# High one-hots and low rows made three steps before their read instead of two, in a ring of eight buffers instead of six

## The chip, the core and the metric

The kernel runs on one core of a Trainium2 chip. A core has five engines that run their own instruction streams and meet only at semaphores: TensorE (PE in the rows; PEld is its loading of weights), VectorE (DVE), ScalarE (ACT), GpSimd (POOL) and SyncE (SP), which here issues most transfers. The metric is the device time of one execution, in microseconds (us).

## The reference

A recommendation model scores 2048 users. Each has 200 history positions with three item ids (below 1000) and one target item.

```python
ub = jnp.concatenate([table_i1[rec_his[:, :, 0]], table_i2[rec_his[:, :, 1]], table_i3[rec_his[:, :, 2]]], axis=2)
mask = rec_his[:, :, 0] == 0
q = jnp.broadcast_to(item_emb[:, None, :], ub.shape)
att_in = jnp.concatenate([q, ub, q - ub, q * ub], axis=-1)
h = att_in @ w_att1.T + b_att1
score = (h @ w_att2.T + b_att2)[..., 0]
score = jnp.where(mask, 0.0, score)
browse = jnp.einsum('bl,ble->be', score, ub)
feat = jnp.concatenate([item_emb, browse, user_emb], axis=-1)
x = _dice(feat @ w1.T + b1, a1, g1, be1)
x = _dice(x @ w2.T + b2, a2, g2, be2)
x = jax.nn.sigmoid(x @ w3.T + b3)
```

The tables have rows of 32 numbers. `_dice` normalises over the whole batch and gates the result.

## The kernel before

**The idea.** No history row is gathered. For a user the score is linear in the looked-up rows, so a table of scores per id is made by matmuls and looked up. An id is split into a high digit (0 to 39) and a low digit (0 to 24). A one-hot matrix of the high digits, multiplied on TensorE with the user's score table, picks 25 candidates per feature; a maximum picks the low digit.

**Tiles, steps, slots.** The batch is cut into 16 tiles of 128 users. A tile is 16 steps of 8 users (16 half-histories of 100 positions), a step is two slots. All loops are over tiles; tile 0 and the last one are written out, VectorE and GpSimd loop over the tiles between, ScalarE and SyncE over pairs of them, TensorE is written out in full. The order on each engine is fixed by hand, and every step n of a tile goes like this:

1. VectorE makes `onehot_hi` (`onehot_high`, L1015: the digits compared with 1 to 40), ScalarE writes eight further columns of the same buffer (`lo_rows`, L902). Both do it for step n + AHEAD while they work on step n; AHEAD is 2.
2. SyncE waits for both, and for a free buffer of `hiT`, and issues a transposing transfer `hiT<-onehot_hi` (`turn_hi`, L336). `hiT` is a ring of four, one per step.
3. TensorE in slot s reads: 24 matmuls `sel<-scoretab,hiT` (`read_scores`, L548). It waits for `hiT`, for the chunk of `scoretab`, and for VectorE and ScalarE to have finished with slot s - 2.
4. VectorE takes maxima (`pick`, L1029), ScalarE makes the low one-hot (`onehot_low`, L883).
5. GpSimd cuts the score into three bf16 parts (`split`, L441 to L457), VectorE multiplies them with the low one-hot (`scale`, L1041).
6. TensorE five slots (LAG) after the read adds up: 24 matmuls `wsum_ps<-scaled_lo,onehot_hi` (`add_scores`, L565). They read the same `onehot_hi` buffer once more, so it comes free only then. ScalarE copies the sums out (L773).

VectorE's order in a step n is pick(2n), one-hot for n + AHEAD, pick(2n + 1), scale(n - 1). In slot s TensorE reads, does one piece of other work if there is one (transposes for the next tile, the first layer, a part of the browse sum, L661), adds for slot s - 5, and then does one piece of the next tile's score tables (L577, L584), for which it waits on ScalarE's copies (L780). Those pieces lie in slots 2 to 10 and 16 to 27.

**The ring before.** `onehot_hi` has six buffers. Steps 0 to 14 use five of them in turn, step 15 has the sixth. Whoever writes a buffer waits until the adds of its last user are done (`wsum_full`, L900 and L1013): at step n this is the add of slot 2n - 5, which TensorE does right after the read of slot 2n.

**SyncE's queue.** Beside the transposes it issues, every two steps, three transfers that place a chunk of the next score table (`place_scores`, L352). The first chunk of tile t + 1 is issued at step 14 of tile t, ahead of the transpose of (t + 1, 0). Every wait of SyncE holds up all that is behind it. In the last tile, at step 11, it issues one load of 1.4 MB (L379).

**Start and end.** VectorE clears `onehot_hi`'s rim (L1098) before it makes `mapq` (L1107), which TensorE needs for the first query; from that hang the first score tables (21 groups of matmuls with a ScalarE copy each, L584, L577 and L780), their placing, and the first read. After the last tile come the statistics and the two layers over the whole batch.

Of the kernel before, what the change touches and what calls it, by code (L numbers as in the profile page):

```python
# [17 lines left out]
def build(nc, r_user, r_item, r_his, table_user, table_i1, table_i2, table_i3, w_att1, b_att1,  # L18
# [22 lines left out]
    STEPS = 16  # L41
    SLOTS = 32
    PER = 16
    RING = 6
    CHUNK = 16
    CHUNKS = TILE // CHUNK
    HELD = 4
# [5 lines left out]
    with ExitStack() as ctx:  # L53
# [15 lines left out]
        weightsum = sb("weightsum", [128, 4, LO, TILE // 4])  # L69
        onehot_hi = sb("onehot_hi", [POSP, RING, PER, HJ], BF16)  # L70
        onehot_lo = sb("onehot_lo", [POS, 2, PER, U], BF16)
# [120 lines left out]
        wsum_full = sem("wsum_full")  # L192
# [24 lines left out]

        def ring_slot(n):

            return n % 5 if n < STEPS - 1 else RING - 1  # L220

        def sums_before(k, n):

            return 2 * k - (8 if 5 <= n < STEPS - 1 else 10 if n < 5 else 2 * STEPS - 2)

        def ring_used(k, n):

            return not isinstance(k, int) or sums_before(k, n) > 0

        prologue = (["attw"] + [("tableT", i) for i in range(7)] + [("digit", 1, 0), ("digit", 0, 0), "item", "query",
                                                                    "w1T", "w1uT", "w2T"])
# [44 lines left out]
                split_at[len(split_at) + (2 if r < 3 else 7)] = (r, piece)  # L278
        SPLIT_DONE = 3 * NR
        LAG = 5  # L280
        AHEAD = 2
        N_SMALL = 2 * NF + 1 + 3 + 8
        EARLY = 3
        assert TILES % 2 == 0
# [6 lines left out]
        def _(sp):  # L291
# [69 lines left out]
            def tile(t, odd, last=False):  # L361
                for n in range(STEPS):
                    if n >= 14 and not last:
                        place_scores(t + 1, n - 14, 1 - odd)
                    if n + AHEAD < STEPS:
                        turn_hi(t, n + AHEAD)
                    elif not last:
                        turn_hi(t + 1, n + AHEAD - STEPS)
                    if n % 2 == 0 and n // 2 + 2 < CHUNKS:
# [373 lines left out]
        def _(act):  # L743
# [143 lines left out]
            def lo_rows(t, n):  # L887

                k = t * STEPS + n
                hb, g0 = n // 8, (n % 8) * PER  # L890
                if n in (0, 8):

                    if isinstance(t, int) and t == 0 and n == 0:
                        act.wait_ge(task_copied, DIGITS0)
                    elif n == 0:
                        act.wait_ge(task_copied, tasks_start(t))
                    else:
                        act.wait_ge(task_copied, task_before(t, 3) + 1)

                if ring_used(k, n):  # L900
                    act.wait_ge(wsum_full, sums_before(k, n))
                act.activation(onehot_hi[0:POS, ring_slot(n), :, 1:1 + 2 * NF],  # L902
                               low_rows[:, hb, g0:g0 + PER, :, :].rearrange("p g j i -> p g (j i)"), ACT.Copy
                               ).then_inc(lo_rows_ready, 1)
# [98 lines left out]
        def _(dve):  # L1003
            def onehot_high(t, n):

                k = t * STEPS + n
                hb, g0 = n // 8, (n % 8) * PER
                if n == 0:
                    dve.wait_ge(task_copied, DIGITS0 - 1 if isinstance(t, int) and t == 0 else tasks_start(t) - 1)
                elif n == 8:  # L1010
                    dve.wait_ge(task_copied, task_before(t, 2) + 1)

                if ring_used(k, n):  # L1013
                    dve.wait_ge(wsum_full, sums_before(k, n))
                dve.tensor_tensor(onehot_hi[0:POS, ring_slot(n), :, HB:].rearrange("p g (j v d) -> p g j v d", j=NF, d=2),  # L1015
                                  digits[:, hb, g0:g0 + PER, :, :].unsqueeze(3)
                                  .to_broadcast([POS, PER, NF, HI // 2, 2]),
                                  iota_hi[:, :].rearrange("p (v d) -> p v d", d=2).unsqueeze(1).unsqueeze(1)
                                  .to_broadcast([POS, PER, NF, HI // 2, 2]),
                                  ALU.is_equal).then_inc(hi_ready, 1)  # L1020
# [194 lines left out]
```

## Time and profile before

| | |
|---|---|
| time, median of 3 runs | 1570.45 us (1567.71 to 1574.2) |
| the profiled execution: time / span | 1565.89 us / 1564.1 us |
| TensorE matmul busy | 1303.5 us, 83% |
| VectorE busy | 1227.8 us, 78% |
| ScalarE busy | 1043.1 us, 67% |
| GpSimd busy | 1006.5 us, 64% |
| TensorE's clock, granted share | 0.941 |
| transfer queue of SyncE (q1) | 162.61 MB, 52.9% of the 16 DMA engines' span |

The profile shows one execution. In its list of groups a row says which line of the kernel, which engine and operation, output and inputs with their shapes, how often, the time busy and the mean of one, and then how long the engine had been idle just before and who released it. The reads begin at 47.2 us and the last one starts at about 1502 us, so 512 slots take 1455 us. An engine's idle time costs something only where it cannot be made up later; with four engines each between 64 and 83% busy, this has to be read place by place.

### The profile page before, as it was taken

Reading aid. Unit: us, or ns where it says so; the run is one execution under the profiler, and the core shown is the slowest. Engines: PE = TensorE matmul, PEld = TensorE weight load, DVE = VectorE, ACT = ScalarE, POOL = GpSimd, SP = SyncE. Lnnn points to the kernel's source line nnn. Section 1 sums busy time; section 2 is a strip of 40 time slices with the busy share of each in tenths; the row PEclk is TensorE's granted clock in tenths of the full one; section 3 lists DMA queues with packets and bytes.
Section 4 is the critical chain, followed back from the end, with each engine's and each line's share of the span. In section 5 each row is a group of like instructions: output and inputs, shape, how many; then the busy total and the mean of one; then the engine's idle time right before and its main releaser. Section 6 shows DMA issues by size and latency. Waiting matters only on the chain.

```text
span 1564.1 us, 67116 instructions
## 1 busy us (share of the span) xinstructions
PE 1303.5 (83%) x27007; PEld 1205.9 (77%) x27007; DVE 1227.8 (78%) x1143; ACT 1043.1 (67%) x2017; POOL 1006.5 (64%) x1671
## 2 busy tenths in 40 slices
PE   5688979879798887989788897989889798988864
PEld 4577868778797876878788787878878797877861
DVE  6588868777878887887877887787788878889845
ACT  6676667766667775676767666676766767775427
POOL 3577657665767766676765766777576666767630
PEclk8899989989999999999989999999999999999976
DMA  3476666566556667666765666667666566766730
GB/s 54 104 143 131 127 117 131 124 131 135 120 127 145 127 131 125 134 135 113 137 137 128 146 127 123 126 147 126 131 144 130 130 125 141 128 129 155 142 69 1
DMA packets 517516, 194.46 MB, mean 124 GB/s; under 512 B 485445, under 2 KB 493237, under 8 KB 517245
## 3 DMA queue, kind: packets, MB, share of 16 engines
q1 hardware_dynamic: 499654, 162.61, 52.9%
q10 hardware_dynamic: 15448, 26.51, 6.8%
q8 instruction: 216, 3.54, 1.0%
q0 software_dynamic: 2144, 1.36, 0.7%
q14 instruction: 54, 0.44, 0.1%
HBM read 8.45 MB, written 1.44 MB: 6 GB/s over the span
## 4 chain that ended last, share of the span: by engine, by line
POOL 47%; issue 27%; PE 10%; ACT 5%; DVE 4%; DMA 3%; POOLq 2%; ACTq 1%; SPq 0%; DVEq 0%
POOL score L443 17%; POOL score L448 8%; POOL score_r L452 7%; POOL parts L456 4%; PE sel L548 3%; POOL parts L453 3%; POOL parts L449 3%; POOL item_rows L421 3%; PE wsum_ps L565 2%; DMA hiT<-onehot_hi 2%; POOL user_rows L429 2%; ACT scores_b L780 2%; PE misc L661 2%; DVE scaled_lo L1041 1%; DVE score_j L1029 1%
## 5 line engine op out<-in xcount | busy, mean ns | idle before, releaser
L883 ACT ACTIVATE onehot_lo<-sel,one 100x600 bf16<-100x600 f32 x512 | 389.0, 760 | 427.7 <-DVE score_j L1029 417.7
L443 POOL TENSOR_TENSOR score<-score_j 100x16 f32<-100x16 f32 x256 | 363.2, 1419 | 396.0 <-DVE score_j L1029 394.0
L548 PE MATMUL sel<-scoretab,hiT 128*128 128x75 bf16 x12288 | 543.6, 203 | 78.5 <-DMA hiT<-onehot_hi 65.6
L548 PEld LDWEIGHTS sel<-scoretab,hiT 128*128 128x128 bf16 x12288 | 509.8, 101 | 123.4 <-DMA hiT<-onehot_hi 70.7
L1029 DVE TENSOR_REDUCE score_j<-sel 100x24 f32<-100x600 f32 x512 | 398.0, 777 | 220.3 <-PE sel L548 217.4
L1041 DVE TENSOR_TENSOR scaled_lo<-onehot_lo,parts 100x3648 bf16<-100x3648 bf16 x256 | 526.3, 2056 | 15.1 <-POOL parts L456 10.4
L565 PE MATMUL wsum_ps<-scaled_lo,onehot_hi 100*128 100x75 bf16 x12288 | 528.3, 201 | 8.6 <-issue 4.4
L565 PEld LDWEIGHTS wsum_ps<-scaled_lo,onehot_hi 100*128 100x128 bf16 x12288 | 488.2, 100 | 15.4 <-issue 5.6
L1015 DVE TENSOR_TENSOR onehot_hi<-digits,iota_hi 100x1920 bf16<-100x1920 bf16 x256 | 297.8, 1164 | 59.1 <-PE wsum_ps L565 56.1
L780 ACT ACTIVATE scores_b<-acc 128x512 bf16<-128x512 f32 (+1 forms) x318 | 255.4, 803 | 35.3 <-issue 18.2
L773 ACT ACTIVATE wsum_ring<-wsum_ps 128x300 f32<-128x300 f32 x512 | 219.9, 430 | 17.1 <-PE wsum_ps L565 16.5
L448 POOL TENSOR_TENSOR score<-score,score_j 100x16 f32<-100x16 f32 x256 | 160.9, 628 | 22.4 <-POOL score L443 0.5
L577 PE MATMUL acc<-scores_b,minus_identb 128*128 128x512 bf16 (+1 forms) x212 | 101.1, 477 | 80.8 <-ACT scores_b L780 80.5
L452 POOL TENSOR_TENSOR score_r<-score,parts 100x16 f32<-100x16 f32 x256 | 145.0, 566 | 20.0
L584 PE MATMUL acc<-queryT,tableT 97*128 97x128 f32 x758 | 117.8, 299 | 40.8 <-ACT scores_b L780 40.8
L584 PEld LDWEIGHTS acc<-queryT,tableT 97*128 97x128 f32 x758 | 99.2, 203 | 45.9 <-ACT scores_b L780 45.8
L456 POOL TENSOR_TENSOR parts<-score_r,parts 100x32 bf16<-100x32 f32 x256 | 107.0, 418 | 20.1
L661 PE MATMUL misc<-weightsum,table_blk 128*96 128x128 f32 x800 | 112.9, 284 | 4.6 <-DMA weightsum<-wsum_ring 4.6
L661 PEld LDWEIGHTS misc<-weightsum,table_blk 128*96 128x96 f32 x800 | 93.3, 167 | 4.8 <-issue 4.8
L577 PEld LDWEIGHTS acc<-scores_b,minus_identb 128*128 128x128 bf16 x212 | 20.6, 97 | 92.6 <-ACT scores_b L780 91.2
L421 POOL DMA_INDIRECT item_rows<-in_L_rec_table_i_dram,ids_now x51 | 70.5, 1383 | 22.2 <-POOL ids_now L415 13.1
L902 ACT ACTIVATE onehot_hi<-low_rows 100x96 bf16<-100x96 bf16 x256 | 74.0, 290 | 0.0
(173 smaller groups left out, 760.6 us busy)
## 6 DMA issues: line engine op xcount, KB each, us to landing
scoretab<-scores_b SPq DMA_DIRECT2D x384, 93.8 KB
weightsum<-wsum_ring ACTq DMA_DIRECT2D x128, 125.0 KB
weightsum<-wsum_ring ACTq DMA_DIRECT2D x64, 150.0 KB
raw<-in_r_rec_his_dram SPq DMA_DIRECT2D x32, 150.0 KB
hiT<-onehot_hi SPq DMA_TRANSPOSE x256, 4.0
x_rows<-x_tile SPq DMA_DIRECT2D x14, 100.0 KB
scores_b<-x_rows SPq DMA_DIRECT2D x1, 1400.0 KB
item_rows<-in_L_rec_table_i_dram,ids_now POOLq DMA_INDIRECT x51
```

What stands on the lines that cost most here:

```text
L443: pool.tensor_tensor(score_2[:, :], score_j[:, p2, :, 0], score_j[:, p2, :, 1], ALU.add).then_inc(parts_step, 1)
L448: pool.tensor_tensor(score[:, :], score_2[:, :], third, ALU.add)
L452: pool.tensor_tensor(score_r[:, :], score[:, :], parts[:, p2, :, 0, 0], ALU.subtract)
L548: mm = pe.matmul(sel[:, 2 * (s % 2) + q, (c % 4) * W:(c % 4 + 1) * W] .rearrange("p (j v) -> p j v", j=NF), hiT[0:HJ, s // 2 % 4, g * POSP ...
L565: mm = pe.matmul(wsum_ps[:, s % 2, b * W:(b + 1) * W].rearrange("p (j v) -> p j v", j=NF), hi_columns(ring_slot(n), g), scaled_lo[:, n % 2 ...
L661: mm = pe.matmul(misc[0:E, 0:TILE].rearrange("p (w b) -> p w b", w=4), table_blk[:, lo, :, :].rearrange("p j e -> p (j e)"), weightsum[0:H ...
L773: act.activation(wsum_ring[:, (s // 8) % 2, :, 4 * (s % 8):4 * (s % 8) + 4], wsum_ps[:, s % 2, 0:4 * W].rearrange("p (b u) -> p u b", b=4) ...
L780: act.activation(scores_b[:, odd, :, stage, slice(*ROUNDS[r])], split_bank(first, r), ACT.Copy).then_inc(split_copied, 1)
L883: act.activation(onehot_lo[:, n % 2, g0:g0 + 8, 0:W].rearrange("p (q c) u -> p q c u", q=2), sel[0:POS, 2 * (s % 2):2 * (s % 2) + 2, 0:4 * ...
L1015: dve.tensor_tensor(onehot_hi[0:POS, ring_slot(n), :, HB:].rearrange("p g (j v d) -> p g j v d", j=NF, d=2), digits[:, hb, g0:g0 + PER, :, ...
L1029: dve.tensor_reduce(score_j[:, n % 2, g0:g0 + 8, :].rearrange("p (q c) j -> p q (c j)", q=2), sel[0:POS, 2 * (s % 2):2 * (s % 2) + 2, 0:4 ...
L1041: ins = dve.tensor_tensor(scaled_lo[:, n % 2, :, :, :].rearrange("p q i (u d) -> p (q i) u d", d=2), onehot_lo[:, n % 2, :, :].unsqueeze(2 ...
```

## The change

The constant AHEAD goes from 2 to 3 and RING from 6 to 8. The ring becomes regular (`n % 8`), and the wait for a free buffer becomes the adds of eight steps back. AHEAD stands in five loops or positions: VectorE's order (L1059 to L1064 and L1120), ScalarE's (L921, L952), SyncE's (L365, L382). Each engine's kinds of instructions stay in the same places; what changes is for which step a one-hot, its low rows and its transpose are. Before tile 0 there are three of each instead of two, and at the end of the last tile three steps without them instead of two. The transposes' own wait for a free `hiT` buffer (L335) is the read of the step before the current one instead of the one before that.

```diff
-    RING = 6
+    RING = 8
...
         def ring_slot(n):
 
-            return n % 5 if n < STEPS - 1 else RING - 1
-
-        def sums_before(k, n):
-
-            return 2 * k - (8 if 5 <= n < STEPS - 1 else 10 if n < 5 else 2 * STEPS - 2)
-
-        def ring_used(k, n):
-
-            return not isinstance(k, int) or sums_before(k, n) > 0
-
-
+            return n % RING
+
+        def ring_used(k):
+
+            return not isinstance(k, int) or k >= RING
...
-        AHEAD = 2
+        AHEAD = 3
...
-                if ring_used(k, n):
-                    act.wait_ge(wsum_full, sums_before(k, n))
+                if ring_used(k):
+                    act.wait_ge(wsum_full, 2 * (k - RING) + 2)
...
-                if ring_used(k, n):
-                    dve.wait_ge(wsum_full, sums_before(k, n))
+                if ring_used(k):
+                    dve.wait_ge(wsum_full, 2 * (k - RING) + 2)
```

VectorE before tile 0, in the kernel before: the clearing of the ring's rim, the first one-hots, the first pick (`score_j<-sel`).

```order
L1098 MEMSET onehot_hi 16x6144
L1099 MEMSET hiT 128x4x8
L1100 MEMSET onehot_lo 100x32
L1103 MEMSET onehot_hi 100x96
L1104 MEMSET onehot_hi 100x96
L1107 TENSOR_SCALAR mapq<-identf,vcol 96x96
L1110 MEMSET scoretab 128x3600 x2
L1116 COPY scoretab<-far 8x16x25 x12
L1015 TENSOR_TENSOR onehot_hi<-digits,iota_hi 100x16x120 x2
L1055 SCALAR_TENSOR_TENSOR digits_b<-raw,digit_hi 128x300
L1029 TENSOR_REDUCE score_j<-sel 100x24
```

The same place in the changed kernel, whose lines stand six lower:

```order
L1092 MEMSET onehot_hi 16x8192
L1093 MEMSET hiT 128x4x8
L1094 MEMSET onehot_lo 100x32
L1097 MEMSET onehot_hi 100x128
L1098 MEMSET onehot_hi 100x128
L1101 TENSOR_SCALAR mapq<-identf,vcol 96x96
L1104 MEMSET scoretab 128x3600 x2
L1110 COPY scoretab<-far 8x16x25 x12
L1009 TENSOR_TENSOR onehot_hi<-digits,iota_hi 100x16x120 x3
L1049 SCALAR_TENSOR_TENSOR digits_b<-raw,digit_hi 128x300
L1023 TENSOR_REDUCE score_j<-sel 100x24
```

The memset grows from 6144 to 8192 elements a partition, ahead of `mapq`, and a third one-hot is made before the first pick.

SyncE from its last load before tile 0 on, in the kernel before: transposes, and the placing of score tables.

```order
L327 DMA raw<-in_r_rec_his_dram 128x300
L336 DMA_TRANSPOSE hiT<-onehot_hi 128x16x112 x2
L352 DMA scoretab<-scores_b 40x1200 x6
L336 DMA_TRANSPOSE hiT<-onehot_hi 128x16x112
L352 DMA scoretab<-scores_b 40x1200 x3
```

And in the changed kernel:

```order
L321 DMA raw<-in_r_rec_his_dram 128x300
L330 DMA_TRANSPOSE hiT<-onehot_hi 128x16x112 x3
L346 DMA scoretab<-scores_b 40x1200 x6
L330 DMA_TRANSPOSE hiT<-onehot_hi 128x16x112
L346 DMA scoretab<-scores_b 40x1200 x3
```

From here on the pattern of the two queues is the same, but each transpose stands for one step later. So where a tile ends, the transpose between the first and second chunk of the next tile's scores is that of its step 1, no longer that of its step 0.

SyncE at the end of the last tile, in the kernel before; `scores_b<-x_rows` is the load of 1.4 MB.

```order
L352 DMA scoretab<-scores_b 40x1200 x3
L336 DMA_TRANSPOSE hiT<-onehot_hi 128x16x112
L379 DMA scores_b<-x_rows 100x2x1792
L336 DMA_TRANSPOSE hiT<-onehot_hi 128x16x112 x2
L392 DMA out_dram<-table_blk 1x2048
```

And in the changed kernel:

```order
L346 DMA scoretab<-scores_b 40x1200 x3
L330 DMA_TRANSPOSE hiT<-onehot_hi 128x16x112
L373 DMA scores_b<-x_rows 100x2x1792
L330 DMA_TRANSPOSE hiT<-onehot_hi 128x16x112
L386 DMA out_dram<-table_blk 1x2048
```

One transpose instead of two stands behind the load.

## Rows read from the trace of the kernel before

**Rows 1.** The page's groups: the one-hots on VectorE.

```profile
L1015 DVE TENSOR_TENSOR onehot_hi<-digits,iota_hi 100x1920 bf16<-100x1920 bf16 x256 | 297.8, 1164 | 59.1 <-PE wsum_ps L565 56.1
```

**Rows 2.** Waits, whole span: us in total, times, longest us.

```profile
DVE score_j L1029 <- PE sel L548: 217.4, 170, 13.9
PE sel L548 <- DMA hiT<-onehot_hi: 65.6, 26, 7.4
...
DVE onehot_hi L1015 <- PE wsum_ps L565: 56.1, 64, 1.8
...
DVE scaled_lo L1041 <- POOL parts L456: 10.4, 23, 1.8
```

**Rows 3.** Timeline where tile 2 begins: start us, us, instruction, [idle before <-releaser].

```profile
217.62 1.74 SPq L336 DMA_TRANSPOSE hiT<-onehot_hi  x1
...
218.68 1.01 PE L548 MATMUL sel<-scoretab,hiT 128*128 128x75 bf16 x24
...
220.37 0.76 ACT L883 ACTIVATE onehot_lo<-sel,one 100x600 bf16<-100x600 f32 x1 [1.52 <-DVE score_j L1029]
...
222.20 2.10 DVE L1041 TENSOR_TENSOR scaled_lo<-onehot_lo,parts 100x3648 bf16<-100x3648 bf16 x1
...
227.77 1.70 PE L548 MATMUL sel<-scoretab,hiT 128*128 128x75 bf16 x24 [7.07 <-DMA hiT<-onehot_hi]
...
229.51 0.78 DVE L1029 TENSOR_REDUCE score_j<-sel 100x24 f32<-100x600 f32 x1 [5.21 <-PE sel L548]
```

**Rows 4.** Timeline where tile 7 begins.

```profile
687.08 0.76 ACT L883 ACTIVATE onehot_lo<-sel,one 100x600 bf16<-100x600 f32 x1 [1.52 <-DVE score_j L1029]
...
689.48 1.61 PE L548 MATMUL sel<-scoretab,hiT 128*128 128x75 bf16 x24 [2.07 <-DMA hiT<-onehot_hi]
...
694.72 0.46 PE L655 MATMUL misc<-item_now,mapq 97*97 97x128 f32 x2 [0.88 <-ACT item_now L827]
```

**Rows 5.** Timeline of VectorE: first pick of tiles 1, 3, 6, 8, 10, 11, 12, 15.

```profile
133.14 0.78 DVE L1029 TENSOR_REDUCE score_j<-sel 100x24 f32<-100x600 f32 x1 [1.15 <-PE sel L548]
...
323.54 0.78 DVE L1029 TENSOR_REDUCE score_j<-sel 100x24 f32<-100x600 f32 x1 [3.73 <-PE sel L548]
...
602.08 0.78 DVE L1029 TENSOR_REDUCE score_j<-sel 100x24 f32<-100x600 f32 x1 [5.76 <-PE sel L548]
...
785.24 0.78 DVE L1029 TENSOR_REDUCE score_j<-sel 100x24 f32<-100x600 f32 x1 [1.88 <-PE sel L548]
...
967.92 0.78 DVE L1029 TENSOR_REDUCE score_j<-sel 100x24 f32<-100x600 f32 x1 [3.12 <-PE sel L548]
...
1057.02 0.78 DVE L1029 TENSOR_REDUCE score_j<-sel 100x24 f32<-100x600 f32 x1 [0.26 <-PE sel L548]
...
1149.20 0.78 DVE L1029 TENSOR_REDUCE score_j<-sel 100x24 f32<-100x600 f32 x1 [0.95 <-PE sel L548]
...
1419.34 0.78 DVE L1029 TENSOR_REDUCE score_j<-sel 100x24 f32<-100x600 f32 x1 [0.82 <-PE sel L548]
```

**Rows 6.** Timeline of the last tile's steps 12 to 14.

```profile
1479.85 1.70 PE L548 MATMUL sel<-scoretab,hiT 128*128 128x75 bf16 x24 [3.46 <-DMA hiT<-onehot_hi]
1480.19 0.86 SPq L379 DMA_DIRECT2D scores_b<-x_rows  x1
...
1481.59 0.78 DVE L1029 TENSOR_REDUCE score_j<-sel 100x24 f32<-100x600 f32 x1 [2.11 <-PE sel L548]
...
1493.29 0.43 PE L565 MATMUL wsum_ps<-scaled_lo,onehot_hi 100*128 100x75 bf16 x4 [4.44 <-issue]
...
1496.28 0.78 DVE L1029 TENSOR_REDUCE score_j<-sel 100x24 f32<-100x600 f32 x1 [4.39 <-PE sel L548]
```

**Rows 7.** The chain that ended last, first 62 us: start us, us, what.

```profile
16.23 5.19 DVE onehot_hi L1098
```

**Rows 8.** The tile hiT over the whole span: time from issue to landing.

```profile
DMA to landing us min/median/max: 3.5/4.0/8.2
```

**Rows 9.** The tile score_r on GpSimd: duration ns min/median/max, first and last start.

```profile
L452 POOL TENSOR_TENSOR score_r<-score,parts x256: 223/226/1219, 52.4 to 1505.8; 100x16 f32<-100x16 f32 x128
```

## The prediction

> **What bounds the kernel now.** I read the waits of the whole span first. TensorE waits 65.6 us in 26 pieces for the transposed one-hots, up to 7.4 us at a time; VectorE waits 56.1 us in 64 pieces, at most 1.8 us each, for TensorE's adds before it may write a one-hot buffer; and VectorE waits 217.4 us for TensorE's reads [rows 2]. The change goes at the first two: the transpose gets a step more of time, and the bigger ring ends the wait for adds (at step n it now asks for slot 2n - 9, long done, where it asked for slot 2n - 5, which TensorE is just doing). The question is which part of them the end of the kernel sees.
>
> Then I read the timeline where a tile begins. In the last steps of a tile TensorE has nothing but reads and adds, and VectorE is the slower of the two. Where tile 2 begins, ScalarE's low one-hot for the last but one slot ends at 220.37 + 0.76 = 221.13; that is what the first read would wait for if nothing else held it. VectorE's last product before it ends at 222.20 + 2.10 = 224.30. But the read starts at 227.77, after 7.07 us of idle time on TensorE, because the transpose issued at 217.62 has only now landed, and VectorE's next pick starts at 229.51, after 5.21 us of idling [rows 3]. So of TensorE's 7.07 us the pipeline pays 5.21: VectorE had work to do for the rest. Where tile 7 begins, the same wait is 2.07 us, and the read could have started at 687.08 + 0.76 = 687.84 instead of 689.48 [rows 4]; there VectorE goes on without a gap that the timeline prints. So a start of a tile costs what VectorE idles before its first pick, not what TensorE idles.
>
> **The change part by part.**
>
> *Tile starts.* The idle times before the first pick are 1.15, 3.73, 5.76, 1.88, 3.12, 0.26, 0.95 and 0.82 at eight starts [rows 5] and 5.21 at tile 2 [rows 3]: 22.9 us. The 0.26 is the largest of the seven small ones; the six others are at most that, 1.1 us by my adding of their rows, so 24.0 us over 15 starts. With the transpose issued a step earlier (VectorE needs 4.77 us of work for a step: two picks of 0.78 [rows 5], a one-hot of 1.16 [rows 1] and a product of 2.05 to 2.10 [rows 3]) its landing moves from 227.77 to about 223 at tile 2 at the latest, ahead of the 224.30 at which VectorE is free. What is late next is VectorE itself. The half-rate clock that comes with the wait goes along with it: the read after the 7.07 us takes 1.70 us and the last one before it 1.01 [rows 3]. I count nothing more for that, since shortly behind the start TensorE waits again, 0.88 us at 694.72, for ScalarE's copy of the item rows, which hangs on the first pick [rows 4]. Bounds: 15 us, if at the two longest starts the next transpose, which now stands in the late one's place, costs back most of their 11 us; 37 us, if VectorE's second wait, before each tile's second pick, goes too (about 0.9 us a start by my reading, worked out like the first). I take 24, which is what the rows of the first pick say alone.
>
> *The transpose that is late next.* At tile 2 the transpose now issued at 217.62 is that of step 1 and lands as before at about 227.7. It is read by slot 2. VectorE's first pick of that tile will start at 224.3, slot 2's read comes after ScalarE's work on slot 0 and the item copies, the query and one read: about 3.9 us later, 228.2. So it fits by half a microsecond. At tile 6 it misses by 0.1 or so. Nothing for these.
>
> *The ring's wait.* Of the 56.1 us I count nothing. The wait ends with an add; TensorE then needs another read of 0.85 us, and mostly a piece of table work too, before VectorE has its next pick, while the one-hot takes 1.16 [rows 1]. So at most 1.16 - 0.85 = 0.3 us of a wait can be seen behind it, 64 x 0.3 = 19 us as the upper end, and only in steps where VectorE is the slower, which are just those without these waits. The lower end is a loss, the third rival below.
>
> *The last tile.* TensorE has no table work there, and VectorE is the slower nearly throughout. VectorE idles 2.11 us at 1481.59 and 4.39 us at 1496.28, both behind a late transpose (3.46 us of idling on TensorE for the first) [rows 6]. The first goes in full. The second stands behind the 1.4 MB load issued at 1480.19, which the transposes of steps 14 and 15 had to follow; that of step 14 now goes ahead of it. But TensorE stops inside an add for 4.44 us until 1493.29, for nothing that the profile shows, while that load runs [rows 6], and this stop may stay. So between 2.1 and 2.1 + 4.4 + about 2 for the waits around them = 8.5; I take 3, near the lower end, because of the stop.
>
> *The start.* The memset of the rim is on the chain that ended last, 5.19 us [rows 7], with `mapq`, the first query and the score tables behind it. It grows by 8192/6144: 5.19 x 1/3 = +1.7 us; the two narrow memsets behind it make that 1.8. The third one-hot (1.16 us [rows 1]) and transpose lie in a stretch where VectorE and SyncE wait for ScalarE's 21 table copies anyway: nothing, or 1.2 us if that cover fails. No instruction is added elsewhere, the one-hots stay at 256 and the transposes at 256.
>
> *Sum.* 1565.9 (the profiled execution's own time; its span is 1564.1) - 24.0 - 3.0 + 1.8 = 1540.7. The median of the runs is 1570.45, 4.6 above the profiled execution. I carry that over: 1545.3, rounded to 1545, a gain of 25.5 us or 1.6%.
>
> **The rivals.**
>
> *All of TensorE's wait comes back.* TensorE is the busiest engine, and the idle time in front of its reads might be worth its full length: 65.6 us [rows 2], so 1570.5 - 65.6 + 1.8 = 1507. For it: at tile 2, 5.21 of 7.07 us do reach VectorE. Against it: at tile 7 nothing of 2.07 does, and seven of the fifteen starts are like it. The Trainium skill's page "Perfetto Trace Analysis", section "Optimization Strategy", says to find the gaps on the most contended engine and make what they depend on start sooner; taken alone it would credit the whole gap and give that time. The rows of VectorE contradict it here.
>
> *The delay is handed on.* The long waits come from transfers that get in each other's way: a landing takes 4.0 us in the middle of the field, 3.5 at least and 8.2 at most [rows 8], and the 8.2 are near the one issued at 217.62, when score chunks and sums move too. The same number of bytes moves after the change, and if the transposes of steps 1 and 2 come late in turn, by more than the slack of 0.5 us worked out above, half or more of the long starts' gain (5.21, 5.76, 3.73, 3.12 and 1.88, 19.7 together [rows 3, 5]) comes back as a wait at slot 2 or 4. With three quarters of it lost: 1545.3 + 15 = 1560; with the last tile's term also lost 1563. For it: slack is small at just the long starts. Against it: a transpose a step later has TensorE's item, query and digit work in front of it. In the Trainium skill, "DMA: Bandwidth & Descriptors", section "Issuing engines are not separate DMA queues", all transfers run on the same 16 DMA engines and interleave, whoever issued them. By that rule an earlier issue buys time to land in and no faster landing, and it is this rival's condition; the spread of 3.5 to 8.2 us agrees.
>
> *Slower: VectorE's earlier one-hot blocks GpSimd.* GpSimd's small operations take 226 ns in the middle of the field and up to 1219 when one of VectorE's wide bf16 operations runs beside them [rows 9]. VectorE's 64 waits are stretches in which GpSimd was free. Once the one-hot starts right after the pick, it may lie on GpSimd's split of the score each time: 64 x 0.99 = 64 us at most on GpSimd. It decides once the parts come later than VectorE's turn to multiply; today it waits for them 10.4 us in all, 23 times [rows 2], so there is slack. If half of the 64 us came through, 1545 + 32 = 1577.
>
> **How the numbers follow.** The forecast has 0.75, with its own range 1536 to 1556 (from the bounds of the terms that I hold likely: 15 to 33 us of gain). All of TensorE's wait: 0.04. The delay handed on: 0.15. Slower: 0.06. The range: below 1533 lie the first rival and a little of the forecast's upper gain, above 1560 half of the second rival and the third, together under 0.2. So 1533 to 1560. About 0.5%, 8 us, is what a measurement of this kernel can tell from no change; faster than 1562.6 come the forecast (nearly whole), the first rival and about a quarter of the second: 0.83; within 0.5% the rest of the second and a bit of the third: 0.11; slower 0.06.
>
> **What would show it.** Right: no wait of TensorE for `hiT` above 1 us at a tile's start, VectorE going from the last product into the first pick of every tile without a gap, VectorE's wait for adds near 0, its wait for reads 217.4 less about 27, the first memset 6.9 us, and the first read at 49.0 instead of 47.2. Wrong: the waits for `hiT` stand at slot 2 or 4 instead (second rival), VectorE's 10.4 us for GpSimd's parts grow past 30 (third), or TensorE's wait for ScalarE's table copies grows by as much as the tile starts give back, in which case the tile was bound there and my reading of the first pick was wrong.

## The result and the profile after

The changed kernel takes 1560.82 us (median, 1547.31 to 1570.7), the one before 1568.34 us on the same chip; the ratio is 0.9939, 95% interval 0.9916 to 0.9962. It is faster by 7.5 us by the medians and by 9.6 us by the ratio. The ratios here and below leave out the executions of either kernel that ran in a slower state, the medians don't. Each ratio is to the kernel before on the same chip. The forecast was 25.5 us faster, and the time lies 0.8 us above the range's upper end. The profiled executions differ less than the medians, 1565.89 before and 1563.67 after, so what follows is about waits that moved more than about a sum. All lines of the changed kernel stand six lower than before (the read is L542, the pick L1023).

Two groups of the changed kernel's page, and then the page of the kernel before for the second of them:

```profile
L1009 DVE TENSOR_TENSOR onehot_hi<-digits,iota_hi 100x1920 bf16<-100x1920 bf16 x256 | 295.5, 1155 | 0.0
...
L446 POOL TENSOR_TENSOR score_r<-score,parts 100x16 f32<-100x16 f32 x256 | 180.2, 704 | 20.0
```

```profile
L452 POOL TENSOR_TENSOR score_r<-score,parts 100x16 f32<-100x16 f32 x256 | 145.0, 566 | 20.0
```

Its waits over the whole span (us in total, times, longest):

```profile
DVE score_j L1023 <- PE sel L542: 282.0, 207, 13.1
...
PE misc L649 <- ACT item_now L821: 42.9, 14, 5.3
...
ACT onehot_lo L877 <- issue: 17.5, 6, 4.6
...
DVE scaled_lo L1035 <- POOL parts L450: 10.2, 31, 1.6
PE sel L542 <- DMA hiT<-onehot_hi: 9.2, 1, 9.2
```

Both waits that the change goes at are gone: VectorE's 56.1 us for the adds are 0.0, and TensorE's 65.6 us for transposes in 26 pieces [rows 2] are one piece of 9.2 in the last tile. Two others stand in their place. TensorE now waits 42.9 us in 14 pieces for `item_now`, ScalarE's copy of the item rows from which the query is made (5.1 us in 7 pieces before). And VectorE waits 282.0 us for reads instead of 217.4: it has made its one-hot earlier, and waits at the next pick instead (with the ring of eight alone, below, this wait is 289.4 us). GpSimd's small operation `score_r` takes 704 ns in the mean instead of 566, so VectorE's earlier one-hot does lie on it, but VectorE's wait for the parts stays at 10.2 us.

The exchange can be counted at the first four picks of tiles 1 to 15. Before them VectorE idled 24.0, 12.9, 1.1 and 10.5 us in all in the kernel before, and 0.0, 2.6, 29.0 and 23.6 us in the changed one: the gaps at the first two picks went and came back at the third and fourth.

The start of tile 12 shows how. Timeline of the changed kernel (start us, us, instruction, idle before and releaser):

```profile
1142.47 1.01 PE L542 MATMUL sel<-scoretab,hiT 128*128 128x75 bf16 x24 [0.66 <-ACT onehot_lo L877]
...
1143.26 2.06 DVE L1035 TENSOR_TENSOR scaled_lo<-onehot_lo,parts 100x3648 bf16<-100x3648 bf16 x1
...
1144.27 1.01 PE L542 MATMUL sel<-scoretab,hiT 128*128 128x75 bf16 x24
1145.23 0.78 DVE L1023 TENSOR_REDUCE score_j<-sel 100x24 f32<-100x600 f32 x1
...
1146.12 0.76 ACT L877 ACTIVATE onehot_lo<-sel,one 100x600 bf16<-100x600 f32 x1 [1.80 <-DVE score_j L1023]
...
1147.45 0.27 ACT L821 ACTIVATE item_now<-misc 96x128 f32<-96x128 f32 x1
...
1147.77 0.74 PE L649 MATMUL misc<-item_now,mapq 97*97 97x128 f32 x2 [2.49 <-ACT item_now L821]
...
1148.31 1.73 PE L559 MATMUL wsum_ps<-scaled_lo,onehot_hi 100*128 100x75 bf16 x24
...
1149.84 1.72 PE L542 MATMUL sel<-scoretab,hiT 128*128 128x75 bf16 x24
...
1151.60 0.78 DVE L1023 TENSOR_REDUCE score_j<-sel 100x24 f32<-100x600 f32 x1 [1.74 <-PE sel L542]
1151.69 1.73 PE L559 MATMUL wsum_ps<-scaled_lo,onehot_hi 100*128 100x75 bf16 x24
```

The first read (1142.47) is early and VectorE goes from its product (ends 1145.32) into the first pick: this is the forecast's picture. But ScalarE's order in slot 0 is the low one-hot (which needs the first pick), and then three item copies; the third ends at 1147.72, and TensorE, which has run ahead to the query of slot 1, stands 2.49 us for it. After it the adds and reads take 1.72 instead of 1.01 us. VectorE has nothing to do then and loses 1.74 us at its third pick. The same stretch in three windows (window, its us, TensorE busy, granted clock, DMA share, GB/s):

```profile
1141.00:1146.00 5.00, 3.62 (x97) 1.00 0.96 214
1146.00:1151.00 5.00, 3.23 (x45) 0.63 0.97 119
1151.00:1156.00 5.00, 5.00 (x77) 0.69 0.37 101
```

The clock falls from its level of 2.4 GHz to that of 1.2 behind the wait. Before, the half clock lay in a tile's first one or two reads (1.70 us in [rows 3]), at the short starts beside VectorE's last product [rows 4]; now it lies in slots 1 and 2, in front of the third and fourth pick. There is not less of it: the mean granted clock is 0.941 before and 0.940 after. What it costs is read from the first reads of four tiles, with tile 4's query in its place:

```profile
412.31 1.01 PE L542 MATMUL sel<-scoretab,hiT 128*128 128x75 bf16 x24 [0.66 <-ACT onehot_lo L877]
...
417.61 0.46 PE L649 MATMUL misc<-item_now,mapq 97*97 97x128 f32 x2 [2.49 <-ACT item_now L821]
...
500.78 1.01 PE L542 MATMUL sel<-scoretab,hiT 128*128 128x75 bf16 x24 [0.66 <-ACT onehot_lo L877]
...
592.70 1.01 PE L542 MATMUL sel<-scoretab,hiT 128*128 128x75 bf16 x24 [0.66 <-ACT onehot_lo L877]
...
1234.69 1.01 PE L542 MATMUL sel<-scoretab,hiT 128*128 128x75 bf16 x24 [0.66 <-ACT onehot_lo L877]
```

Tile 4, whose clock did not fall, takes 500.78 - 412.31 = 88.5 us. Tile 12 has the same wait of 2.49 us in front of its query, its clock fell (10.2 us of the tile are at half clock), and it takes 1234.69 - 1142.47 = 92.2; tile 5, with a fall and a longer wait (3.58 us), takes 91.9. So the fall costs some 3.7 us a tile here. Of tiles 1 to 14, only 4 and 8 were spared it. Tile 6 has no wait for the item copy in the list: TensorE stops there for 3.80 us inside the read before the query, for nothing that the profile shows, and its clock falls as well.

From tile 3 on, where an odd tile begins, ScalarE adds a standstill of its own. Tile 7 of the changed kernel:

```profile
687.74 0.78 DVE L1023 TENSOR_REDUCE score_j<-sel 100x24 f32<-100x600 f32 x1
...
691.47 0.76 ACT L877 ACTIVATE onehot_lo<-sel,one 100x600 bf16<-100x600 f32 x1 [4.64 <-issue]
...
693.12 0.74 PE L649 MATMUL misc<-item_now,mapq 97*97 97x128 f32 x2 [5.33 <-ACT item_now L821]
```

Its input, the first pick, had ended at 687.74 + 0.78 = 688.52, 2.95 us earlier. That is the standstill; the rest of the 4.64 us is the ordinary wait for the pick. The profile names no releaser ("issue"). It is there at each of the six turns of ScalarE's loop over pairs of tiles (tiles 3, 5, 7, 9, 11 and 13), where the low one-hot starts 1.20 to 2.95 us behind its input, 10.7 us in all, and 0.11 us behind it at the even tiles.

It was there before the change too. Tile 7 of the kernel before, where the low one-hot starts 1.16 us behind the end of the pick:

```profile
691.13 0.78 DVE L1029 TENSOR_REDUCE score_j<-sel 100x24 f32<-100x600 f32 x1
...
693.07 0.76 ACT L883 ACTIVATE onehot_lo<-sel,one 100x600 bf16<-100x600 f32 x1 [3.16 <-issue]
```

Last, the two ends of the kernel. Of the chain that ended last, the piece that answers to [rows 7] and one in the last tile; then the timeline of the latter's surroundings:

```profile
17.26 6.89 DVE onehot_hi L1092
...
1476.44 16.55 DMA hiT<-onehot_hi
```

```profile
1476.44 2.12 SPq L330 DMA_TRANSPOSE hiT<-onehot_hi  x1
...
1478.75 0.85 SPq L373 DMA_DIRECT2D scores_b<-x_rows  x1
...
1493.04 1.70 PE L542 MATMUL sel<-scoretab,hiT 128*128 128x75 bf16 x24 [9.22 <-DMA hiT<-onehot_hi]
...
1494.78 0.78 DVE L1023 TENSOR_REDUCE score_j<-sel 100x24 f32<-100x600 f32 x1 [8.40 <-PE sel L542]
```

The memset grew by 1.70 us as worked out, but the first read came 3.3 us later (50.50 instead of 47.22). In the runs below that keep the large memset ahead of `mapq` it came at 49.05 to 49.77. In the last tile the wait before step 12's pick is gone, and the 2.11 and 4.39 us of [rows 6] have become 8.40 in one piece, before step 14's: its transpose now goes out 2.3 us ahead of the 1.4 MB load, as worked out, and lands only after 16.55 us. From its first read to the start of its last one the tile still took 2.1 us less than before (81.64 instead of 83.76).

### The profile page after: what moved, and what is told of

It reads as the page before. It is cut to its first block, busy times and chain, and to the rows that moved or that the text cites. A ratio compares the mean times of both kernels' runs of the same rounds, so it can differ in the third digit from the quotient of the medians.

```text
span 1561.9 us, 67018 instructions
## 1 busy us (share of the span) xinstructions
PE 1298.1 (83%) x27007; PEld 1200.5 (77%) x27007; DVE 1222.3 (78%) x1143; ACT 1047.3 (67%) x2017; POOL 1066.5 (68%) x1671
## 4 chain that ended last, share of the span: by engine, by line
POOL 59%; issue 25%; PE 5%; ACT 3%; DVE 2%; POOLq 2%; DMA 2%; ACTq 1%; SPq 0%; DVEq 0%
POOL score L437 23%; POOL score_r L446 11%; POOL score L442 7%; POOL parts L450 5%; POOL parts L447 4%; POOL parts L443 4%; POOL item_rows L415 4%; POOL user_rows L423 2%; PE sel L542 1%; DMA hiT<-onehot_hi 1%; ACT scores_b L774 1%; PE wsum_ps L559 1%; PE misc L655 1%; DVE score_j L1023 1%; POOLq L435 1%
## 5 line engine op out<-in xcount | busy, mean ns | idle before, releaser
L437 POOL TENSOR_TENSOR score<-score_j 100x16 f32<-100x16 f32 x256 | 409.0, 1598 | 335.5 <-DVE score_j L1023 334.8
L1023 DVE TENSOR_REDUCE score_j<-sel 100x24 f32<-100x600 f32 x512 | 398.4, 778 | 284.5 <-PE sel L542 282.0
L542 PE MATMUL sel<-scoretab,hiT 128*128 128x75 bf16 x12288 | 536.4, 202 | 38.8 <-ACT onehot_lo L877 17.0
L542 PEld LDWEIGHTS sel<-scoretab,hiT 128*128 128x128 bf16 x12288 | 503.6, 100 | 83.5 <-issue 62.7
L1035 DVE TENSOR_TENSOR scaled_lo<-onehot_lo,parts 100x3648 bf16<-100x3648 bf16 x256 | 525.5, 2053 | 13.5 <-POOL parts L450 10.2
L446 POOL TENSOR_TENSOR score_r<-score,parts 100x16 f32<-100x16 f32 x256 | 180.2, 704 | 20.0
L442 POOL TENSOR_TENSOR score<-score,score_j 100x16 f32<-100x16 f32 x256 | 115.6, 452 | 22.4 <-POOL score L437 0.5
L415 POOL DMA_INDIRECT item_rows<-in_L_rec_table_i_dram,ids_now x51 | 73.7, 1445 | 22.2 <-POOL ids_now L409 13.1
L447 POOL TENSOR_TENSOR parts<-score,parts 100x32 bf16<-100x32 f32 x256 | 78.7, 307 | 0.0
```

Of the source, the lines that this page charges most:

```text
L437: pool.tensor_tensor(score_2[:, :], score_j[:, p2, :, 0], score_j[:, p2, :, 1], ALU.add).then_inc(parts_step, 1)
L442: pool.tensor_tensor(score[:, :], score_2[:, :], third, ALU.add)
L446: pool.tensor_tensor(score_r[:, :], score[:, :], parts[:, p2, :, 0, 0], ALU.subtract)
L542: mm = pe.matmul(sel[:, 2 * (s % 2) + q, (c % 4) * W:(c % 4 + 1) * W] .rearrange("p (j v) -> p j v", j=NF), hiT[0:HJ, s // 2 % 4, g * POSP ...
L1023: dve.tensor_reduce(score_j[:, n % 2, g0:g0 + 8, :].rearrange("p (q c) j -> p q (c j)", q=2), sel[0:POS, 2 * (s % 2):2 * (s % 2) + 2, 0:4 ...
L1035: ins = dve.tensor_tensor(scaled_lo[:, n % 2, :, :, :].rearrange("p q i (u d) -> p (q i) u d", d=2), onehot_lo[:, n % 2, :, :].unsqueeze(2 ...
```

## The experiments

Theory 1: the waits for transposes did cost the 24 us that the first picks show, and the changed kernel gives them back at the next thing that is late, ScalarE's item copy, together with the half clock behind it and ScalarE's standstill. Rivals: the larger ring brings something by itself; the earlier one-hot harms GpSimd; the starts were never worth 24 us.

**Item copies first.** In slot 0 of a tile ScalarE makes its three item copies ahead of the low one-hot.

```diff
-                onehot_low(t, s)
+                if s > 0:
+                    onehot_low(t, s)
...
+                if s == 0:
+                    onehot_low(t, s)
```

> The changed kernel (three steps ahead, ring of eight), with one edit: in slot 0 of a tile ScalarE copies the item rows before it makes the low one-hot, so before VectorE's first pick instead of behind it. Theory 1 (the wait was handed on: TensorE now waits 42.9 us in 14 pieces at the query for ScalarE's item copy, and runs slots 1 to 3 at half clock behind that wait): the query wait falls under 10 us, tiles take about 88 us instead of 92, the time is 1560.8 - 14 x 3.5 = about 1512 us. Theory 2 (VectorE's earlier one-hot blocks GpSimd, the query is beside the point): 1555 to 1562. Theory 3 (TensorE is bound by table work behind the start whatever the query does): the wait moves to slots 3 and 4, ScalarE's table copies, 1550 to 1560.

Measured: 1542.21 us (1537.29 to 1547.29), ratio to the kernel before 0.9844 (0.9789 to 0.9899). Waits:

```profile
PE misc L649 <- ACT item_now L821: 20.3, 6, 4.0
...
ACT item_prev L816 <- issue: 20.0, 6, 4.0
```

The wait for the copy is gone at even tiles and stays at the odd ones, where ScalarE stands still at its loop's turn. Theory 1 has the place right; the size it expected (about 1512 us) was too large. The standstill was still there, and in this execution tiles 3, 5, 6, 7, 9 and 13 still lost the clock.

**The same edit in the kernel before.**

> The kernel before (two steps ahead, ring of six) with the same edit: item rows copied before the low one-hot of slot 0. Theory 1: there the item can only be transposed after the late first read, so the copy comes earlier only by a pick and a low one-hot (0.8 + 0.8 us less the copy's own way): 0 to 1.5 us a tile, 1568 - 0 to 20 us. If it gains as much as on the changed kernel, the query wait was a matter of its own and the change is worth nothing beside it.

1562.53 us, ratio 0.9963 (0.9915 to 1.001). Without the change the item copy's place is worth nothing that can be told; the waits for the transpose are still there (56.9 us in 23 pieces).

**The two halves of the change.** The ring of eight alone (AHEAD stays 2), and three steps ahead with a ring of eight whose writers still wait as those of six buffers would.

```diff
-        AHEAD = 3
+        AHEAD = 2
```

> Ring of eight, still two steps ahead: the ring's part alone. Theory 1: VectorE's 56 us of waits for adds go and nothing comes of it; the start costs 2 to 3 us, so 1568 + 0 to 3. Theory 2 (GpSimd blocked by the earlier one-hot): slower by 10 to 30 us, GpSimd's busy time up from 1006 towards 1066. If the ring's wait was worth what it lasted: faster by 20 us or more.

1567.65 us, ratio 0.9974 (0.9934 to 1.0013). VectorE's wait for adds is 0 there, its wait for reads 289.4 us and TensorE's wait for transposes 70.5 us in 27 pieces: the ring's 56.1 us went over to the reads and were worth nothing that can be told, as forecast.

```diff
-            return not isinstance(k, int) or k >= RING
+            return not isinstance(k, int) or k >= 6
...
-                    act.wait_ge(wsum_full, 2 * (k - RING) + 2)
+                    act.wait_ge(wsum_full, 2 * (k - 6) + 2)
...
-                    dve.wait_ge(wsum_full, 2 * (k - RING) + 2)
+                    dve.wait_ge(wsum_full, 2 * (k - 6) + 2)
```

> Three steps ahead, ring of eight, but the writers still wait for the add of slot 2n - 5 as before (eight buffers, of which two are never used early). Theory 1: as the changed kernel, 1558 to 1563. Theory 2: GpSimd's busy time back to about 1006 and 10 to 30 us faster than the changed kernel, 1530 to 1550.

1560.13 us, ratio 0.9948 (0.9914 to 0.9983): as the changed kernel, with VectorE waiting 62.7 us for adds and GpSimd busy 1027 us instead of 1066.5. So the third step ahead has the whole gain without the ring's wait being gone, and GpSimd's longer operations cost nothing that can be told. The interval of the ring alone overlaps the changed kernel's, so that the ring adds nothing at all is not shown.

**Extra matmuls.** The changed kernel with 16 matmuls whose results nobody uses, ahead of the query in slot 1.

```diff
+                if s == 1 and t > 0 and s in here:
+                    for i in range(FILL):
+                        pe.matmul(acc[:, 0:4 * W], identb[:, :], scoretab_flat[:, 0:4 * W], start=True, stop=True)
```

> The changed kernel with 16 extra matmuls (identity by 300 columns, into a PSUM bank that nobody uses there) between the second read of a tile and the query, where TensorE waits for ScalarE's item copy: work added, nothing removed. Theory 1 with the clock as its second half (the idle before the query drops TensorE to 1.2 GHz for slots 1 to 3, which costs 2.8 us a tile): the granted clock stays up at the tiles that start an even tile, those tiles take 88.4 us and not 92, and the kernel with more work is faster, 1560.8 - 8 x 3 = about 1537. If the half clock is a bystander: 1560 to 1565.

1540.49 us (1537.68 to 1544.16), ratio 0.9806 (0.9762 to 0.985). Where tile 7 begins:

```profile
672.33 2.21 PE L680 MATMUL acc<-scoretab,identb 128*128 128x300 bf16 x16
...
674.56 0.76 ACT L881 ACTIVATE onehot_lo<-sel,one 100x600 bf16<-100x600 f32 x1 [3.02 <-issue]
...
676.21 0.46 PE L650 MATMUL misc<-item_now,mapq 97*97 97x128 f32 x2 [1.67 <-ACT item_now L825]
...
678.82 1.73 PE L560 MATMUL wsum_ps<-scaled_lo,onehot_hi 100*128 100x75 bf16 x24
```

And its waits:

```profile
PE misc L650 <- ACT item_now L825: 14.1, 13, 3.4
```

More work made it 20 us faster by the medians. The wait in front of the query fell from 42.9 to 14.1 us, by 28.8, but the fillers that took its place are 14 x 2.21 = 31 us: the item copy comes no earlier for them, and by the waits alone nothing is won. What changed is the clock behind it. At even tiles it did not fall, and they take 88.4 to 89.1 us; at this odd one 1.67 us of waiting were left and it still did (1.73 for an add). Of tiles 1 to 14 four lost the clock instead of twelve, and the mean granted clock is 0.963 instead of 0.940. Eight falls fewer at 3.7 us are 30 us; the two profiled executions differ by 26.0. So this run tells the clock from the wait itself, and the clock is most of what the moved wait costs.

**The query matrix ahead of the memset**, on top of item copies first:

```diff
+            act.wait_ge(rim_zero, 1)
...
+            dve.wait_ge(vcol_ready, 1)
+            dve.wait_ge(const_ready, 2)
+            dve.tensor_scalar(mapq[0:E, 0:E], identf[0:E, 0:E], vcol[:, 1:2], None, ALU.mult).then_inc(mapq_ready, 1)
...
-            dve.wait_ge(vcol_ready, 1)
-            dve.wait_ge(const_ready, 2)
-            dve.tensor_scalar(mapq[0:E, 0:E], identf[0:E, 0:E], vcol[:, 1:2], None, ALU.mult).then_inc(mapq_ready, 1)
```

> item_first (1542.2) plus VectorE making mapq ahead of the memset of the one-hot ring's rim. My term for the start was the memset's growth of 1.7 us on the chain, and the changed kernel's first read stood at 50.5 us against 47.2. Theory: the memset leaves the chain, the first read comes at 45.5 to 47, and 1538 us. If the memset was not what held the first read, it stays at 49 to 50.

1540.44 us, ratio 0.9811 (0.9764 to 0.9858). The memset left the chain and the first read came at 46.48 instead of 49.37 us, but a gain of 2.9 us cannot be told from none by these intervals.

**Table work one slot later**, on top of that:

```diff
-        EVERY = {0: "item", 1: "query", 2: ("digit", 1, 1), 3: ("digit", 0, 1), FIN_SLOT + PARTS - 1: "finish",
+        EVERY = {0: "item", 2: "query", 3: ("digit", 1, 1), 4: ("digit", 0, 1), FIN_SLOT + PARTS - 1: "finish",
...
-                split_at[len(split_at) + (2 if r < 3 else 7)] = (r, piece)
+                split_at[len(split_at) + (3 if r < 3 else 7)] = (r, piece)
```

> mapq_first plus the query, the two digit tasks and the first nine table pieces one slot later, so that ScalarE's item copy has a slot more. Theory 1: the query wait, 20.3 us in 6 pieces in item_first, halves or better, with the half clock behind it, 1525 to 1532. Rival (what TensorE waits for is ScalarE as a whole behind a tile's start): the wait only changes its line, to the query's or the table copies, 1538.

1592.38 us, ratio 1.0126 (1.008 to 1.0171): slower than the kernel before, by 52 us slower than the kernel that it was built on, and outside both expectations. TensorE's wait for the item copy is gone, but its waits for low one-hots and table copies grew and the mean granted clock is 0.930, where it was 0.953:

```profile
PE acc L578 <- ACT scores_b L774: 65.4, 45, 2.5
PE sel L542 <- ACT onehot_lo L877: 39.5, 50, 3.7
```

They were 42.6 and 19.7 us in the kernel that it was built on. Two things were moved together, the query and the table pieces behind it; which of them costs this, and why the clock fell so often, stays open.

**ScalarE's loop written out**, with item copies first, and alone.

```diff
-            with act.Fori(0, TILES // 2 - 1) as pair:
+            for pair in range(TILES // 2 - 1):
```

> item_first with ScalarE's loop over pairs of tiles written out. Theory: the six query waits left (tiles 3, 5, 7, 9, 11, 13, where ScalarE begins a new turn of its loop and stands still up to 4.0 us for nothing the profile shows) are that loop's branch: 20.3 us goes to under 4, 1542 - 6 x 5 = about 1515 with the half clock's share. If the standstill stays, it is not the branch: 1542.

With item copies first: 1529.47 us (1523.97 to 1532.27), ratio 0.9734 (0.9691 to 0.9778). ScalarE's unexplained pieces at the tile starts and TensorE's wait for the item copy are both gone at odd tiles too. The theory had the place right; its 1515 us were not reached. Where tile 12 begins:

```profile
1114.70 1.01 PE L542 MATMUL sel<-scoretab,hiT 128*128 128x75 bf16 x24
...
1115.43 0.27 ACT L821 ACTIVATE item_now<-misc 96x128 f32<-96x128 f32 x1
1115.72 0.78 DVE L1026 TENSOR_REDUCE score_j<-sel 100x24 f32<-100x600 f32 x1
1115.76 0.46 PE L649 MATMUL misc<-item_now,mapq 97*97 97x128 f32 x2
1116.05 0.99 PE L559 MATMUL wsum_ps<-scaled_lo,onehot_hi 100*128 100x75 bf16 x24
```

> The changed kernel with ScalarE's loop over tile pairs written out and nothing else; the item task stays behind the low one-hots. Theory 1 (the standstill at the loop's turn costs the six odd starts up to 5 us of the query's wait, while the item copy's place costs all starts 2.5 us and the half-rate clock behind it): the odd starts become like the even ones, the query's wait falls from 42.9 to 32 to 35 us in 14 or 15 pieces of about 2.4, clock stretches stay: 1550 to 1556. Rival (the standstill was the whole of it): 1530 to 1535, like the version with both edits.

Alone: 1536.9 us (1533.13 to 1544.17), ratio 0.9816 (0.9755 to 0.9877). The wait is as theory 1 said, the time is not:

```profile
PE misc L649 <- ACT item_now L821: 32.5, 14, 2.5
```

Every start of tiles 1 to 14 but tile 6's waits 2.46 or 2.47 us, and the time is 24 us below the changed kernel's, where I had expected 5 to 11. It lies nearer to the rival's 1530 to 1535. In its profile nine of the fourteen starts of tiles 1 to 14 lost the clock, in the changed kernel's twelve; 3 x 3.7 us and the 10.4 us less of waiting are 21.5, and the two profiled executions differ by 19.5 us. The wait being the same everywhere, this run prices the fall once more: tiles 5, 7, 10 and 12, spared it, take 88.0 to 88.3 us, and tiles 1, 2, 3, 8, 9 and 13, which were not, 91.7 to 93.1 (4 and 14, with shorter falls, 90.0 and 89.4). The same wait of 2.5 us thus brings the clock down at some starts and not at others, and what decides between them stays open. Whether the item copy's place is worth anything once the loop is written out (0.9816 without it, 0.9734 with it) the intervals do not tell.

**The worth of the change with the obstacles gone.** The kernel before with both edits of ScalarE:

> The kernel before with two edits of the changed kernel's best version: ScalarE does slot 0's item task ahead of its table of low one-hots, and its loop over tile pairs is written out. Ring of six, two steps ahead, as before. Theory 1 (the change does remove some 25 us of waits at tile starts, and ScalarE's late item copy and its standstill at the loop's turn then take them back): with both out of the way the change shows its full worth, so this kernel stands 20 to 27 us above the 1529 of the changed kernel with the same edits, 1550 to 1556. Rival (the two edits are what gains, and the change is worth its 7.5 us with them as without): 1535 to 1540.

1564.35 us (1552.02 to 1575.75), ratio 0.9967 (0.9921 to 1.0012), against 0.9734 (0.9691 to 0.9778) with the change. Its waits:

```profile
PE sel L548 <- DMA hiT<-onehot_hi: 71.0, 27, 7.8
```

The two edits are worth nothing that can be told without the change, and the change is worth 1564.35 - 1529.47 = 35 us with them, 37 by the two ratios. Theory 1 expected 20 to 27; the rival (7.5 us as without them) is out. The gaps say where the rest is: before the first and the second picks of tiles 1 to 15 VectorE idles 29.7 and 13.5 us in this kernel, and 0.0 and 1.1 us in the changed one with the same edits, and nothing comes back at the third and fourth (7.3 us and 4.0 us). The profiled executions of the two differ by 43.7 us.

**The best version**, all three edits, and the same with the extra matmuls.

> The changed kernel with three edits: item task first in ScalarE's slot 0, ScalarE's loop over tile pairs written out, and VectorE's small query matrix made ahead of the memset of the ring's rim. Theory 1: the loop's 1529.5 less the 2.9 us by which the first read came earlier in the version without unrolling (49.37 to 46.48): 1525 to 1528. Rival (the start's gain is lost as it was there, where the time fell by 1.8 of 2.9 and within its interval): 1529 to 1530.

1524.9 us (1515.4 to 1529.11), ratio 0.9738 (0.9659 to 0.9816): the lowest median, some 41 us below the kernel before by the ratio, though the ratio is the same as without the third edit.

> The same with the sixteen extra matmuls of 300 columns ahead of the query in slot 1 of each tile after the first; they compute nothing that is used. They gained 20 us where TensorE stood 2.5 us there. With the item copy early that wait is gone, and what is left of TensorE's idle time at a tile start is 2 us behind slot 2's product, which the filler does not fill. Theory 1: the filler now costs its own 2.1 us at each of 15 starts less what it spares of half-rate clock, so 1535 to 1555, slower than without it. Rival (the filler holds the clock up whatever the wait): 1515 to 1525.

1526.88 us, ratio 0.9747 (0.9671 to 0.9823), the same as without them. I had expected a loss of 10 us or more and it is not there; nor is a gain. Where the wait is gone, extra matmuls have nothing left to save. Why they cost nothing either, 14 x 2.2 = 31 us of work on the busiest engine, stays open.

## Why the prediction was wrong

*What bounds the kernel, and the first picks.* Right as far as it goes. VectorE goes from the last product into the first pick without a gap at all fifteen starts, and with ScalarE out of the way the change is worth 35 us. The gaps before the second picks, 12.9 us by the trace and counted only in the upper bound of 37, went as well; 24 was the lower part of what could be had.

*The step that failed* is in "Tile starts": "What is late next is VectorE itself", and with it "I count nothing more for that, since shortly behind the start TensorE waits again, 0.88 us at 694.72, for ScalarE's copy of the item rows, which hangs on the first pick". The row was read and its meaning missed. A wait that hangs on the first pick does not move with TensorE: if TensorE comes earlier by the whole wait for the transpose, and the pick only by VectorE's own gap, the difference is added to the 0.88. That happened: 65.6 us of waiting for transposes went to 9.2, and 5.1 us of waiting for the item copy went to 42.9. Nor was the 0.88 the pick's alone: ScalarE stood still for 1.16 us there. And I priced the first picks alone; the gaps before the third and fourth grew by 41 us in all, from 11.6 to 52.6. The forecast's last sentence comes near, but names the wrong copy: TensorE's waits for the table copies went from 121.3 to 126.0 us only.

*The half clock* was the size that I set to nothing, on the ground that it goes along with the wait. It did not go: the mean granted clock is 0.941 before and 0.940 after. It costs some 3.7 us at a start where it falls in slots 1 and 2, and the extra matmuls, which take most of it away and bring the item copy no earlier, bring 20 us.

*ScalarE's standstill* is no term of the forecast: in the kernel before, it was up to 1.16 us, and the written-out loop gains nothing that can be told there, so what it costs came with the change. In the Trainium skill, "Runtime: NRT & Kernel Launch", section "Instruction fetch mechanics", a taken branch whose target isn't at hand makes the engine wait for its instructions. The runs agree: ScalarE starts 1.20 to 2.95 us behind its input at each of the six turns, and at most 0.04 us behind it at every tile start when the loop is written out. That its cause is the fetching itself no run here shows.

*The ring's wait*: nothing, right (ratio of the ring alone 0.9974, 0.9934 to 1.0013). But the sign "wait for reads 217.4 less about 27" left out that this wait goes over to the reads: it rose to 282.0. *The start*: the memset's 1.70 us were right; the first read moved by 3.3 in this execution, not 1.8. The memset began 1.03 us later than before, which I cannot put down to the change, and 0.55 us stay unexplained. The third one-hot doesn't explain them: with the ring alone, which has two, 2.55 - 0.50 - 1.70 = 0.35 us are over as well. In the other runs the first read came at 49.05 to 49.77, near the forecast 49.0. *The last tile*: forecast 3 us of gain; VectorE's two gaps of 6.5 us became one of 8.4, and the tile's reads took 2.1 us less in all. *The forecast's own range*: 15 to 33 us of gain off 1570.45 are 1537.5 to 1555.5, not 1536 to 1556; nothing hangs on it.

*The rivals.* "The delay is handed on" gave 1560 to 1563, and the time is 1560.8. That number is luck: no transpose is late at slot 2 or 4, it is ScalarE's copy at slot 1. GpSimd's operations did grow (its busy time by 60 us), and nothing that can be told came of it: that rival is out. All of TensorE's wait coming back (1507) did not happen.

## What to carry to other kernels

When a wait is taken away, list what the waiting engine meets next, and for each piece ask what it hangs on. If that releaser does not move along, the new wait is as long as the engine has moved ahead of it, and it may lie where nothing covers it. Price idle time on TensorE with the half clock behind it, in the place where it falls, and not only with its length. Edits that are worth nothing by themselves (here the item copy's place and the written-out loop, in the kernel before) can be what another one needs.

## What the runs showed of the hardware

- 16 extra matmuls, 2.21 us of work at each of 14 tile starts, made the kernel 20 us faster than the changed one: TensorE's idle time in front of the query became shorter, and its mean granted clock is 0.963 instead of 0.940.
- ScalarE stands still at its loop's turn, for up to 2.95 us behind its input, six times; written out, its loop takes 24 us off the changed kernel. In the kernel before, with the item copies first, it takes nothing off that can be told.
- The same wait of about 2.5 us lowers the clock at some tile starts and not at others; a tile takes 88.5 us in the one case and 92.2 in the other.
- What half clock costs depends on its place, and the mean clock does not rank the kernels: the changed kernel with both edits of ScalarE has 0.951 and is 11 us faster than the one with the extra matmuls and 0.963. In the former, tile 5 has 6.8 us at half clock some 65 us behind its start and takes 88.9 us, tile 2 has none and takes 87.8.
- A transpose issued 2.3 us ahead of a 1.4 MB load took 16.55 us to land instead of 3.9 (the middle of the field), and TensorE waited 9.22 us for it. In the nine other runs with this order of issues it took 14.8 to 14.9 us in five and 5.1 to 5.9 in four, and in all nine TensorE stopped for 2.75 to 7.64 us inside an add next to that read, for nothing that the profile shows, as it does in [rows 6]. So going first in the queue saved the transpose in some runs only, and an early landing did not save TensorE's stop.
